# Turning 8 of 128 key blocks of attention weights per batch by VectorE squares and DMA in place of TensorE

## What is computed

```python
h = maximum(layernorm(x), 0)                       # x: (16, 1024, 512)
q, k, v = h @ Wq + bq, h @ Wk + bk, h @ Wv + bv     # 8 heads of 64
scores = einsum('bihd,bjhd->bhij', q, k) / 8 + where(adj == 0, -1e9, 0)
out = einsum('bhij,bjhd->bihd', softmax(scores, axis=-1), v)
return x + out
```

## Time and profile before

| | us |
|---|---|
| median of 3 runs | 3953.45 (3953.0 to 3953.62) |
| the profiled execution, its own time | 3952.87 |
| span of that profile | 3951.1 |
| PE busy | 3925.2 (99%) |
| DVE busy | 3109.3 (79%) |
| ACT busy | 3010.7 (76%) |
| POOL busy | 1389.6 (35%) |
| one batch, from V(121) to V(121) of the next | 245.2 |

### The profile page before, as it was taken

The page is one execution under the profiler, slowest core; times in us unless marked ns, Lnnn a source line. Parts: engine busy times, 40 slices in busy tenths (PEclk is TensorE's granted clock), DMA queues, the critical chain, the costliest instruction groups (busy, mean ns, idle before and its releaser), DMA issues.

```text
span 3951.1 us, 64302 instructions
## 1 busy us (share of the span) xinstructions
PE 3925.2 (99%) x21504; PEld 3219.8 (81%) x21504; DVE 3109.3 (79%) x5263; ACT 3010.7 (76%) x5386; POOL 1389.6 (35%) x1399
## 2 busy tenths in 40 slices
PE   8999999999999999999999999999999999999998
PEld 7888888888888888888888888888888888888887
DVE  7878878788787887878878788787887868878687
ACT  6877868778686886868868688686886868868687
POOL 4334333343333333333333333333333333334322
PEclk9999999999999999999999999999999999999999
DMA  6233333333323333334233342332433324324232
GB/s 208 60 88 72 88 78 67 85 79 80 83 66 83 89 70 84 73 75 95 63 84 80 68 96 65 82 84 62 96 73 75 87 61 94 80 67 90 51 76 49
DMA packets 722325, 316.44 MB, mean 80 GB/s; under 512 B 629840, under 2 KB 629840, under 8 KB 713424
## 3 DMA queue, kind: packets, MB, share of 16 engines
q1 hardware_dynamic: 722000, 312.34, 34.7%
HBM read 173.28 MB, written 38.27 MB: 54 GB/s over the span
## 4 chain that ended last, share of the span: by engine, by line
PE 92%; DVE 6%; issue 1%; ACT 1%; POOL 0%; DMA 0%; ACTq 0%; POOLq 0%; DVEq 0%
PE T L604 21%; PE misc L558 16%; PE S L589 11%; PE O L623 11%; PE S L590 11%; PE O L616 11%; PE misc L571 9%; DVE pT L909 2%; DVE S L903 1%; PE misc L537 1%; DVE bn L869 1%; DVE qB L886 1%; DVE y L928 0%; DVE qA L886 0%; ACT pT L722 0%
## 5 line engine op out<-in xcount | busy, mean ns | idle before, releaser
L909 DVE TENSOR_TENSOR pT<-T,pT 128x512 fp32r<-128x512 f32 x2048 | 1378.7, 686 | 657.1 <-ACT pT L722 651.5
L722 ACT CAST pT<-T 128x512 fp32r<-128x512 f32 x2048 | 1187.1, 590 | 412.8 <-PE T L604 326.1
L903 DVE CUSTOM_DVE_ANT_0 S<-S,mask 128x1024 f32<-128x1024 f32 x1024 | 1251.9, 1223 | 1.2 <-PE S L590 1.2
L604 PEld LDWEIGHTS T<-ident,probs 128*128 128x128 f32 x8192 | 996.9, 140 | 301.8 <-DVE pT L909 64.4
L604 PE MATMUL T<-ident,probs 128*128 128x128 f32 x8192 | 1236.5, 273 | 4.6 <-DVE pT L909 0.5
L741 ACT ACTIVATE probs<-S,negmax 128x1024 f32<-128x1024 f32 x1024 | 1150.7, 1124 | 7.0 <-DVE negmax L903 3.8
L623 PE MATMUL O<-pT,vs 128*64 128x512 f32 x2048 | 954.5, 466 | 0.2 <-DVE pT L909 0.2
L616 PE MATMUL O<-pT,vs 128*128 128x512 f32 x2048 | 816.1, 398 | 0.0
L558 PE MATMUL misc<-hT,wqk 128*128 128x512 f32 x3036 | 734.3, 391 | 0.0
L456 POOL TENSOR_TENSOR outs<-outs,oT 64x512 f32<-64x512 f32 x255 | 338.2, 1326 | 1024.4 <-DMA outs<-oT 1021.1
L558 PEld LDWEIGHTS misc<-hT,wqk 128*128 128x128 f32 x3036 | 570.0, 188 | 122.0 <-issue 0.2
(11 more groups left out here) (78 smaller groups left out, 3298.9 us busy)
## 6 DMA issues: line engine op xcount, KB each, us to landing
wqk<-wqk_split SPq DMA_DIRECT2D x63, 1024.0 KB, 6.0
xln<-in_x SPq DMA_DIRECT2D x240, 256.0 KB, 2.7
kA<-kA SPq DMA_DIRECT2D x128, 256.0 KB, 3.2
kB<-kB SPq DMA_DIRECT2D x128, 256.0 KB, 3.8
outs<-in_x SPq DMA_DIRECT2D x256, 128.0 KB, 3.6
outs<-oT SPq DMA_DIRECT2D x256, 128.0 KB, 3.6
out<-outs SPq DMA_DIRECT2D x252, 128.0 KB, 3.3
rinv_sq<-rinv_turned SPq DMA_DIRECT2D x512, 2.0 KB, 1.7
```

The costliest lines, as they stand in the source:

```text
L604: mm = pe.transpose(T[:, u % 2, i * P:(i + 1) * P], probs[:, (GB * g + i) % RING, j * P:(j + 1) * P], ident[:])
L722: act.copy(pT[:, u % PT, 0, :], T[:, u % 2, :]).then_inc(p_hi, 1)
L903: dve.tensor_tensor_reduce(S[:, s % 2, :], S[:, s % 2, :], mask[:, s % NB, :], 1.0, 3.0e38, ALU.add, ALU.min, negmax[:, s % RING:s % RING ...
L909: dve.tensor_tensor(pT[:, u % PT, 1, :], T[:, u % 2, :], pT[:, u % PT, 0, :].bitcast(F32), ALU.subtract).then_inc(p_lo, 1)
```

## The change

Eight units per batch are no longer turned by PE: 125 and 126 of a batch, and 2 to 7 of the next. The first batch has only 125 and 126, the last only 2 to 7, so that 15 batch boundaries have eight each. They go in packs of two, `PACKS` = (unit at which DVE turns, first unit of the pack): (0, 6), (121, 125), (126, 2 of the next batch), (127, 4 of the next batch). For a pack:

- DVE, behind `probs_low` of the unit `at`, turns 128x1024 elements in squares of 32x32, `turn_pack`, from `probs` into `xln` (the other place, `wv_squares`, would be taken for `at` from 2 to 120, which no pack has). It waits for the exponentials and for the complete store of the pack before (`sq_out`).
- SP stores it to DRAM with four DMAs, one for each 32 partitions, `store_pack`, at unit `at`. At unit `at + 1` it waits for them and loads the two units back over the untransposed blocks in `probs`, squares now in place, with two DMAs, `load_pack`.
- ACT and DVE read the unit from `probs` in SBUF in place of `T`, `probs_hi` after `exponential` where both are due.

The load of the first tiles into `xln` goes from unit 0 to unit 1 and waits for the pack of unit 0 to be stored. One half of the V weights is stored to DRAM once and loaded back at unit 110 of every batch.

```diff
+PACKS = ((0, 6), (121, 125), (126, 130), (127, 132))
+TWO = 2
+XLN_AT = 1
+WV_FREE, WV_AT = 2, 110
...
+            def store_pack(b, k, at):
+                n, src = pack_no(b, k), squares(at)
+                sp.wait_ge(sq_turned, n + 1)
+                if some(n - 1):
+                    for i in range(TWO):
+                        sp.wait_ge(sq_in[i], 16 * (n - 1))
+                for a in range(QUADS):
+                    dst = turned_dram[n % 2, :, :, a, :].rearrange("j c n -> c j n")
+                    sp.dma_start(dst, src[a * SQ:(a + 1) * SQ]).then_inc(sq_out, 16)
+
+            def load_pack(b, k, slot):
+                n = pack_no(b, k)
+                sp.wait_ge(sq_out, 16 * QUADS * (n + 1))
+                for i in range(TWO):
+                    src = turned_dram[n % 2, QUADS * i:QUADS * (i + 1)].rearrange("q c a n -> (q c) a n")
+                    sp.dma_start(probs_of(UNITS * b + slot + i), src).then_inc(sq_in[i], 16)
...
+                    if u == XLN_AT and not first and not last:
+                        sp.wait_ge(h_turned, NB * (b + 1))
+                        sp.wait_ge(sq_out, 16 * QUADS * pack_no(b, len([at for at, _ in PACKS if at < WV_FREE])))
+                        for t in range(XLN):
+                            load_xln(b + 1, t)
...
             def turn_probs(b, u):
 
                 n, g, j = UNITS * b + u, u // NB, u % NB
+                if pack_of(b, u):
+                    return
...
             def probs_hi(b, u):
                 n = UNITS * b + u
-                act.wait_ge(turned, n + 1)
+                moved = pack_of(b, u)
+                if moved:
+                    act.wait_ge(sq_in[moved[1]], 16 * (moved[0] + 1))
+                else:
+                    act.wait_ge(turned, turned_to(n))
...
             def probs_low(b, u):
-                dve.wait_ge(p_hi, UNITS * b + u + 1)
-                dve.tensor_tensor(pT[:, u % PT, 1, :], T[:, u % 2, :], pT[:, u % PT, 0, :].bitcast(F32),
-                                  ALU.subtract).then_inc(p_lo, 1)
+                n = UNITS * b + u
+                dve.wait_ge(p_hi, n + 1)
+                if pack_of(b, u):
+                    hi, lo = (pT[:, u % PT, i, :].rearrange("p (t a r) -> p a t r", t=GB, a=QUADS) for i in (0, 1))
+                    dve.tensor_tensor(lo, probs_of(n).rearrange("p a (t r) -> p a t r", r=SQ), hi.bitcast(F32), ALU.subtract).then_inc(p_lo, 1)
...
+            def turn_pack(b, k, at, slot):
+                n, pack = UNITS * b + slot, pack_no(b, k)
+                dve.wait_ge(exped, GB * (n // NB + 1))
+                if some(pack):
+                    dve.wait_ge(sq_out, 16 * QUADS * pack)
+                else:
+                    dve.wait_ge(wv_out, 16)
+                dve.transpose(squares(at).rearrange("p j (t r) -> p t j r", r=SQ),
+                              probs_of(n, TWO).rearrange("p t (j c) -> p t j c", c=SQ)).then_inc(sq_turned, 1)
...
                     probs_low(b, u)
+                    for k, at, slot in packs_of(b):
+                        if u == at:
+                            turn_pack(b, k, at, slot)
```

More of the change, by code:

```diff
@@ L89, with packs_of, pack_no, pack_of @@
 SPREAD_0 = (2, 2, 6, 6, 6, 6, 8, 8)
+PACKS = ((0, 6), (121, 125), (126, 130), (127, 132))
+TWO = 2
+XLN_AT = 1
+WV_FREE, WV_AT = 2, 110
 W_ORDER = ((1, 0), (0, 0), (0, 1), (0, 2), (0, 3), (1, 1), (1, 2), (1, 3))
 XLN_USES = [len(range(r, NB, XLN)) for r in range(XLN)]
+def packs_of(b):
+    return [(k, at, slot) for k, (at, slot) in enumerate(PACKS)
+            if (b < B - 1 or at < (PAIRS - 1) * PER) and (b > 0 or at >= WV_FREE)]
+def pack_no(b, k):
+    return len(PACKS) * b + k - len([at for at, _ in PACKS if at < WV_FREE])
+def pack_of(b, u):
+    for k, at, slot in packs_of(b):
+        if slot <= u < slot + TWO:
+            return pack_no(b, k), u - slot
+    if b > 0:
+        for k, at, slot in packs_of(b - 1):
+            if slot <= u + UNITS < slot + TWO:
+                return pack_no(b - 1, k), u + UNITS - slot
+    return None
+MOVED = [[u for u in range(UNITS) if pack_of(b, u)] for b in range(B)]
+def turned_to(n):
+    b, u = divmod(n, UNITS)
+    return n + 1 - sum(len(MOVED[i]) for i in range(b)) - len([s for s in MOVED[b] if s <= u])
 def some(n):
@@ L122, in adj_preln_kernel @@
         kB = sb("kB", [P, 2, 2, N], F32R)
+        with nc.sbuf_tensor("wv_squares", [P, TWO * QUADS, P], F32) as wv_squares:
+            pass
         wv = sb("wv", [P, 2, C, D], F32R)
@@ L193, in adj_preln_kernel @@
         y_scaled, y_added = sem("y_scaled"), sem("y_added")
+        sq_turned, sq_out, sq_in = sem("sq_turned"), sem("sq_out"), [sem(f"sq_in{i}") for i in range(TWO)]
         rinv_out, rinv_in, tail_done = sem("rinv_out"), sem("rinv_in"), sem("tail_done")
@@ L331, in body @@
                     p, v = u // 32, u % 32
-                    if u == 0 and not first and not last:
-                        sp.wait_ge(h_turned, NB * (b + 1))
-                        for t in range(XLN):
-                            load_xln(b + 1, t)
                     if u % NB == LAG and not (first and u == LAG):
@@ L371, in body @@
                         load_wqk((p + 2) % PAIRS)
+                    for k, at, slot in packs_of(b):
+                        if u == at:
+                            store_pack(b, k, at)
+                    if u == WV_AT and not last:
+                        load_wv(b)
             body(0, first=True)
@@ L566, in project_v @@
                 pe.wait_ge(*free)
-                if isinstance(b, int) and b == 0:
+                if b == 0:
                     pe.wait_ge(wv_split, 1)
+                elif j == 0:
+                    pe.wait_ge(wv_in, 16 * b)
                 parts = [(c, wl, hl) for c in range(C) for wl, hl in ((0, 0), (1, 0), (0, 1))]
@@ L596, in turn_probs @@
                 n, g, j = UNITS * b + u, u // NB, u % NB
+                if pack_of(b, u):
+                    return
                 if j == 0:
                     pe.wait_ge(exped, GB * (GROUPS * b + g + 1))
-                if some(n - 1):
-                    pe.wait_ge(p_lo, n - 1)
+                last = n - 2
+                while last >= 0 and pack_of(*divmod(last, UNITS)):
+                    last -= 2
+                if last >= 0:
+                    pe.wait_ge(p_lo, last + 1)
                 else:
@@ L727, in exponential @@
                 if some(free):
-                    act.wait_ge(turned, free)
+                    act.wait_ge(turned, turned_to(free - 1))
+                    moved = [m for m in range(free - NB, free) if pack_of(*divmod(m, UNITS))]
+                    if moved and s % GB == 0:
+                        act.wait_ge(p_lo, moved[-1] + 1)
                 if n == 0:
@@ L835, in body @@
                         copy_out(b, u // NB - 1)
-                    probs_hi(b, u)
+                    moved = pack_of(b, u)
+                    if not moved:
+                        probs_hi(b, u)
                     s = u // 2 + LEAD - 1
```

30 lines of the change are left out of this document (29 added, 1 removed).

## The result

The changed kernel takes 3968.3 us (median of 5 runs, 3965.8 to 3972.4) against 3953.0 for the kernel before beside it: 1.004 times as long, 95% interval 1.0025 to 1.0054. The profiled execution took 3966.7, with a span of 3964.9; the clock was granted in full (0.998). So the change loses 15 us (0.4%), where I forecast a gain of 25 (0.6%), and the time lies above the range of 3908 to 3966.

What follows compares the result with a forecast made beforehand. PE was taken to set the pace around the V projections; 3.48 us of turns saved less 1.75 of waits, 1.73 us at 15 boundaries, gave 26 us: 3928 us against the median before, range 3908 to 3966.

Steps and rivals of the forecast that it cites:

- Eight turns, 3.48 us per boundary: PE at each of 15 batch boundaries: eight turns saved at 0.435 us each, 52 us in all.
- DVE's room: Up to the middle of unit 9: DVE busy 9.66 of 15.47 us, 5.8 us of room for added work.
- I count nothing for both: High parts from SBUF (0.2 us per boundary) and low parts (1.2 us) were taken as hidden by ACT's and DVE's room.
- rival 2: Units 2 to 8: two-SBUF-input low parts, slowed beside POOL, exceed DVE's room; loss 1.1 us per boundary, 3969; chance 0.07.
- The waits for stores, 1.75 us per boundary: Transposes at units 127 and 0 await the previous store, so PE waits before V(0) and V(1), 1.75 us together.
- my 1.35: Before V(0): PE's predicted wait for `bias_v(127)`, behind the second transpose and `shift`, 1.35 us.
- L: Time from a transpose's end to its four stores' complete landing: taken as 4.5 us, bounds 4.2 and 5.54.
- my formula: PE's waits before V(0) and V(1): (L - 3.15) and (L - 4.1), together 2L - 7.25, or 1.75 us.
- Rival 1: Third transpose: second store held up by a 512 KB load, 2.2 us; 3960 to 3990; chance 0.2, near 3965.
- The transpose: 1.24 us: DVE's transpose of 128x1024, four per boundary: 1.24 us each, between bounds of 1.22 and 1.42.
- High parts, other DMAs at nothing: ACT's high parts from SBUF (617 against 590 ns) and delays of `move_o` and other DMAs were taken to cost nothing.
- The sum: Per boundary: 3.48 us saved less 1.75 of waits gains 1.73, times 15 is 26 us.

Runs made afterwards that it cites:

- e2: Changed kernel without the packs' transposes, stores and loads, the eight units reading whatever `T` holds (wrong values): 3913.9 us, ratio 0.9902.
- e4: Changed kernel with the eight low parts subtracting from the stale `T` in PSUM instead of `probs` (wrong values): 3936.5 us, ratio 0.9959.
- e5: Changed kernel with only the two packs turned at units 121 and 126: 3934.8 us, ratio 0.9954.
- e3: Changed kernel with PE's turns and PSUM reads kept, transposes and stores done for nothing, loads left out: 3980.2 us, ratio 1.0071.
- e1: Changed kernel with SP storing a pack ahead of loading the pack before: 3974.3 us, ratio 1.0054.
- e13: Changed kernel with stores ahead of loads and the last group's `move_o` at unit 1: 3963.7 us, ratio 1.0023.
- e14: Changed kernel with only the last group's `move_o` moved, from unit 2 to unit 1: 3963.4 us, ratio 1.0021.
- e8: Changed kernel with POOL's sum of group 14 moved from unit 125 to 127: 3948.7 us, ratio 0.9989.
- e10: Changed kernel with only the packs of units 121 and 126, and POOL's sum moved from unit 125 to 127: 3935.8 us, ratio 0.9956.

## Why the prediction was wrong, step by step

- **Eight turns, 3.48 us per boundary.** 2.55 arrived (e2). The bias addition limits the V gaps (0.39 lost), a wait that only e2 has takes 0.37, and DVE's full stretch of units 9 to 16 the last 0.19. So 2.9 is nearer to what the turns are worth. I had read DVE's room in the earlier trace rows only as far as unit 9, where it ends.
- **Low parts: "I count nothing for both."** This step failed: 2.14 us per boundary, 32 us (after - e4). The rows for it were on the table: the earlier trace rows has the maximum of 1673 ns, the mean of 834, and I read the mean as a price of 0.15 us that room absorbs. It isn't a price of 0.15 each but one of up to 1.1 for some, at fixed places, and these places have no room: unit 125, from which a row of dependent steps leads to V(0) (1.30, with the late stores in it), and units 6 and 7 beside POOL's sum, `kA` and `kB` (1.14, with `qA`'s share). It is my rival 2, in mechanism and in units 2 to 8, but priced for there alone and given 0.07. The Trainium skill, "SBUF — State Buffer", section "Who interferes with whom", has the rule: a DVE instruction with two SBUF inputs contends with a GpSimd instruction that reads SBUF, and one with at most one SBUF input, outside the modes that use two ports, doesn't. The traces agree in both halves (1.46 us beside a POOL addition and 1.67 beside a subtraction; 0.69 for the low part from PSUM in e5, and 1.24 for the transpose at 1025.00, which has one input, beside the POOL row at 1024.96).
- **The waits for stores, 1.75 us per boundary.** Mechanism right: DVE's queue, `shift`, `bias_v`, PE; in after V(0) waits 1.32 (2.52 less a gap of 1.20) and V(1) 0.70, 2.02 in all. That the first is so near to my 1.35 is luck: with the true L my formula gives 0.63, and the typical boundary has 0.9; the held-up low part and three late stores make up the rest. Without them the same waits are 0.23 and 0.87 (e4), 1.10. With all that transposes and stores cost elsewhere this part is 1.54 (e4 - e2) or, with PE's turns kept, 1.7 (e3 - before). L is 3.78 us for a store alone and typically 4.8 behind a load, where I had 4.5 for both; issuing four stores took 1.83 us and not 2.7.
- **Rival 1, the second store held up behind the load.** It exists: 1 us typically (4.8 against 3.78, and 3.8 again where e1 and e3 have no load ahead). The 2.2 that I had priced is seen at 1031 alone (6.0), and 1.2 us of it only beside the packet of the instruction queue. But e1 and e13 show that undoing it gains nothing: what V(1) doesn't wait, the units behind it do.
- **The transpose: 1.24 us.** 1.241.
- **High parts, other DMAs at nothing.** ACT's high part from SBUF took 0.61, as thought, and ACT waited 0.5 us for loads in all. `move_o`'s delay is perhaps 5 us (e14), not settled.
- **The sum.** -3.48 + 1.75 = -1.73 was forecast; measured are -2.55 + 1.54 + 2.14 = +1.13. Had the low parts cost nothing, the other two terms would have made a gain of 1.01, near 3938, in the forecast's own range, though with a saving a quarter smaller than mine; e4 has 3936.5.
- **The advice of the Trainium skill to turn 128x128 tiles with TensorE if PSUM will do** ("VectorE: DVE Perf Modes", section "Rules for kernel authors") holds for the change as it was, and not for its half: e5 turns four of the blocks with DVE and is 0.5% faster.

Open is what part of the 0.12 and 0.87 us of e4 - e2 is DVE's time and what the wait (the high parts from SBUF and their place behind the exponential are in there, too), how much of the changed kernel's time `move_o` has, and what makes single stores late.

## What to carry to other kernels

When an edit moves an operand from PSUM to SBUF, look in the trace at what GpSimd runs at the very places of the new instructions, and which of the two starts first; price a meeting by the maximum of the nearest row, not by its mean. An average of busy time is no cover for an instruction at the head of a row of dependent steps, and a bounding engine relieved in one stretch wins only what the next stretch's engines can follow: read the windows until one is full. Try the half of a change that has no wait in it first. And when a test kernel puts an old operand back, ask which waits come back with it.

## What was unexpected of the hardware

- DVE's subtraction with both inputs in SBUF, started beside a running POOL `tensor_tensor`, ended 0.55 us after POOL's end, to within 0.01, in all the 44 cases of after that were held up: as if most of its 0.69 us came behind. Started ahead of it, it was never held up, and POOL's 1.29 us became 1.61 to 1.77 in the cases shown.
- A store of 512 KB in four pieces from 32 partitions each let the next transpose start 3.78 us after the transpose's end, and typically 4.8 with a load of 512 KB issued 1.35 us ahead of it. All 9 of 60 that landed later than 4.9 us had a packet of 16 KB of the instruction queue beside them.
- One POOL instruction moved by two units was worth 20 us (e8), and nothing where no store wait followed (e10).
